# Softmax tails stacked high over low by DMA: two tail passes of 128 rows for three of 104 in a cross-attention and mixture-of-experts kernel

## The chip, the core and the metric

The kernel runs on one core of a Trainium2 chip. Five engines of the core work side by side, each through its own list of instructions, and meet only at semaphores: TensorE (PE) multiplies and transposes, VectorE (DVE) and ScalarE (ACT) read PE's results out of PSUM, GpSimd (POOL) works from SBUF alone, and SyncE (SP) issues the DMA transfers. The metric is the time of one launch on the device in microseconds, the median of three runs.

## What is computed

A layer norm and a cross-attention of 2x1024 rows of width 256 over 154 context rows, with 16 heads of 64, and then a soft mixture of 16 experts with 64 slots each. The part that the change touches is the attention:

```python
q = (x_q @ Wq + bq).reshape(b, sq, H, D_HEAD).transpose(0, 2, 1, 3)
k = (x_k @ Wk + bk).reshape(b, sk, H, D_HEAD).transpose(0, 2, 1, 3)
v = (x_v @ Wv + bv).reshape(b, sk, H, D_HEAD).transpose(0, 2, 1, 3)
s0 = jnp.einsum('bhqd,bhkd->bhqk', q, k) / math.sqrt(D_HEAD)
s0 = jnp.where(mask_mat, NEG, s0)
p = jax.nn.softmax(s0, axis=-1)
s1 = jnp.einsum('bhqk,bhkd->bhqd', p, v)
return s1.transpose(0, 2, 1, 3).reshape(b, sq, D_MID) @ Wo + bo
```

After it the feed-forward part takes a softmax over rows and one over slots of the same logits, runs a gated two-layer network in each expert, and adds the combined result to x.

## The kernel before

**Split operands.** Every matrix is held as two fp32r halves, the rounded value ("high") and what the rounding left ("low"). A product is three passes: high by high, low by high, high by low (`PASSES`, `LEFT_LAST`). For each result in PSUM ACT writes the high half into SBUF, DVE subtracts it from the PSUM value and writes the low half, and that frees the PSUM bank.

**Steps of the attention.** The 2048 rows are 8 groups of 256 rows. The 16 heads are 8 pairs, two pairs make a quad, and a step n is one group with one quad: 8 groups of 4 quads are 32 steps. The events of a step, (name, n, ...), stand in `STEP`, and the queue of PE follows it: S00 to S11 (scores of a pair and a row tile; L1461), Q0, Q1 (queries of the next step; L1439), T0, T1, T2 (transposes of the probabilities of step n-1), PV0, PV1 (probabilities by values of step n-2, one event for each pair), and once in four steps xT and Y0, Y1, the product with Wo (48 matmuls, L1369). R0 and R1 are a reciprocal on DVE and two multiplications on POOL. The tables `LATER_DVE`, `LATER_ACT`, `LATER_POOL` move an event by so many places in that engine's queue; `EARLY` puts single pieces of work ahead of a named event: the projections of keys ("K", pair), of values ("V", batch, half), of the value tails ("VT", half), and the splits of the weights.

**Tails.** A head has 154 keys: 128 and a tail of 26. The main parts of a head's probabilities go through T0 and T1 as 128x128 transposes. The tails of the four heads of a quad go together: `prob_t` holds 4x26 = 104 columns, T2 transposes them (L1479), ACT and DVE write the halves `pT[0]` and `pT[1]` (tile 4), and in each PV event three of the nine matmuls (L1501) multiply `vt`, the value tails of the quad with the other heads' columns at zero, by them: 104 rows each, high by high, low by high, high by low.

**SP's queue.** SP issues its DMAs in one order: first the loads in `LOADS`; then, as they come up, the key blocks of pairs 2 to 7 (L607, two DMAs each, `kbd<-keys`) and, after the last value tail ("VT", 1), eight DMAs that spread the value tails into `vt` (L600, four for each batch); then the second batch's x (L609), the two norm vectors (L610, L611) and, after the last V event, Wo (L614), 1 MB each for x and Wo. Each DMA waits on SP only for what stands ahead of it. The first PV event waits for the first batch's four `vt` transfers (L1492). After that SP has nothing to do in the attention until the slot embeddings are loaded half way through (L617).

## Time and profile before

| | us |
|---|---|
| three runs, median (lowest to highest) | 544.42 (544.23 to 544.68) |
| profiled execution, time / span from first to last instruction | 544.24 / 542.5 |
| PE, PE weight load, DVE, ACT, POOL busy | 530.0, 499.8, 434.1, 402.2, 303.3 |
| load and projections, up to the first Y | 0 to 66 |
| steady attention | 66 to 262 |
| end of the attention, second norm | 262 to 296 |
| logits, slots, experts, combine | 296 to 542.5 |

The time of a launch is the span and 1.7 us around it. A busy share counts an engine as at work from the start of an instruction to its modelled end; what the order of the work costs is read from the chain of waits, which goes back from the last instruction to what released it, and from the rows on what PE waited for.

### The profile page before, as it was taken

To read this page: it belongs to the slowest core of one execution; us is meant where nothing else is said; L and a number is where in the kernel's file an instruction comes from. 1 tells how busy PE (TensorE), PEld (TensorE's weight loads), DVE (VectorE), ACT (ScalarE), POOL (GpSimd) and SP (SyncE) were. 2 spreads that over 40 slices of the span, in tenths; PEclk is the share of its full clock that TensorE was granted. 3 is DMA by queue.
4 is the path that set the end of the run, shared out by engine and by line. 5 is a ranking of instruction groups with operands and counts; after the bars stand their busy time and mean duration, and the time that the engine had idled before them with its cause. 6 is when DMAs were issued, how large, how long until landed. Compare 5 with 4: busy or idle time off the path is not lost.

```text
span 542.5 us, 11967 instructions
## 1 busy us (share of the span) xinstructions
PE 530.0 (98%) x3896; PEld 499.8 (92%) x3896; DVE 434.1 (80%) x1305; ACT 402.2 (74%) x1098; POOL 303.3 (56%) x327
## 2 busy tenths in 40 slices
PE   6999999999999999999998999999999999999997
PEld 4889999999999999999997888999978888899997
DVE  6777878787897979899677998798699888865453
ACT  5879969596896959779564555788979889766562
POOL 6674654544545455454365768787467999910000
DMA  8635000000030000000001333150288888525551
GB/s 257 181 86 179 3 1 2 2 2 1 3 98 2 2 2 1 2 0 4 0 1 80 155 156 156 78 201 1 79 264 283 270 306 288 182 79 170 181 167 67
DMA packets 34901, 54.11 MB, mean 100 GB/s; under 512 B 3997, under 2 KB 21497, under 8 KB 34713
## 3 DMA queue, kind: packets, MB, share of 16 engines
q1 hardware_dynamic: 34841, 53.36, 29.7%
q8 instruction: 32, 0.52, 0.4%
q14 instruction: 28, 0.23, 0.1%
HBM read 40.54 MB, written 10.49 MB: 94 GB/s over the span
## 4 chain that ended last, share of the span: by engine, by line
PE 90%; ACT 4%; DMA 2%; POOL 1%; DVE 1%; issue 1%; SPq 0%; ACTq 0%; DVEq 0%
PE ps L1461 9%; PE ps L1585 9%; PE ps L1357 9%; PE ps L1369 8%; PE ps L1610 8%; PE ps L1499 8%; PE ps L1439 7%; PE ps L1552 7%; PE ps L1476 5%; PE ps L1632 4%; PE ps L1501 4%; PE ps L1644 3%; DMA wvo_raw<-in_L_xattn_Wo_dram 2%; ACT expo L885 1%; PE ps L1615 1%; PE ps L1622 1%
## 5 line engine op out<-in xcount | busy, mean ns | idle before, releaser
L885 ACT ACTIVATE expo<-expo,nmin 128x154 f32<-128x154 f32 x256 | 106.2, 423 | 5.3 <-DVE nmin L1135 4.8
L1135 DVE CUSTOM_DVE_ANT_0 expo<-ps,maskb 128x154 f32<-128x154 f32 x256 | 69.1, 312 | 11.9 <-PE ps L1461 11.9
L723 POOL TENSOR_TENSOR prob_t<-expo,prec 128x104 f32<-128x104 f32 x64 | 23.1, 360 | 89.3 <-DVE prec L1146 89.1
L726 POOL TENSOR_TENSOR prob<-expo,prec 128x512 f32<-128x512 f32 x64 | 66.8, 1043 | 0.0
L1461 PE MATMUL ps<-kbd,qT_high 128*128 128x308 f32 x256 | 61.1, 323 | 0.0
L1155 DVE TENSOR_TENSOR pT_low<-ps,pT_high 128x512 fp32r<-128x512 f32 (+1 forms) x96 | 57.2, 596 | 4.1 <-ACT pT_high L899 3.9
L788 POOL TENSOR_TENSOR w_gu_low<-w_raw,w_gu_high 128x1024 fp32r<-128x1024 f32 x17 | 50.3, 2966 | 16.2 <-ACT w_gu_high L835 16.1
L899 ACT CAST pT_high<-ps 128x512 fp32r<-128x512 f32 (+1 forms) x96 | 49.1, 513 | 10.8 <-PE ps L1476 8.1
L803 ACT ACTIVATE oT_high<-ps,bqv_c 128x256 fp32r<-128x256 f32 x64 | 29.8, 466 | 34.8 <-PE ps L1501 34.7
L885 ACT ACTIVATION_READ_ACCUMULATOR expo<-expo,nmin 128x1 f32 x256 | 50.3, 196 | 0.0
L1461 PEld LDWEIGHTS ps<-kbd,qT_high 128*128 128x128 f32 x256 | 39.8, 190 | 0.2
L1461 PE MATMUL ps<-kbd,qT_low 128*128 128x308 f32 x128 | 39.0, 304 | 0.0
L1476 PE MATMUL ps<-ident,prob 128*128 128x128 f32 x256 | 38.5, 273 | 0.1
L1369 PE MATMUL ps<-wvo_high,oT_high 128*128 128x256 f32 x128 | 37.0, 289 | 0.0
L1501 PE MATMUL ps<-pT_high,vt 104*128 104x256 f32 x128 | 36.3, 284 | 0.0
L1369 PE MATMUL ps<-wvo_high,oT_low 128*128 128x256 f32 x128 | 36.2, 283 | 0.0
L1369 PE MATMUL ps<-wvo_low,oT_high 128*128 128x256 f32 x128 | 36.0, 281 | 0.0
L1357 PE MATMUL ps<-eo_high,comb 128*128 128x256 f32 x256 | 34.6, 287 | 0.4 <-issue 0.4
L1032 DVE SCALAR_TENSOR_TENSOR oT_low<-ps,bqv_c,oT_high 128x256 fp32r<-128x256 f32 x64 | 30.3, 474 | 5.3 <-ACT oT_high L803 4.5
L922 ACT COPY lsb<-ps 128x512 f32<-128x512 f32 x32 | 17.2, 589 | 22.3 <-PE ps L1552 22.3
L1006 ACT CAST comb<-ps 128x512 fp32r<-128x512 f32 x32 | 17.2, 590 | 21.3 <-PE ps L1644 21.3
L1032 DVE SCALAR_TENSOR_TENSOR qT_low<-ps,bqv_c,qT_high 128x256 fp32r<-128x256 f32 x64 | 29.9, 468 | 3.7 <-ACT qT_high L803 3.6
(241 smaller groups left out, 1762.7 us busy)
## 6 DMA issues: line engine op xcount, KB each, us to landing
logits_dram<-lsb SPq DMA_DIRECT2D x16, 512.0 KB, 2.6
w_raw<-in_L_ffn_Wg_dram SPq DMA_DIRECT2D x16, 512.0 KB, 4.0
w_raw<-in_L_ffn_Wu_dram SPq DMA_DIRECT2D x16, 512.0 KB, 4.5
w_raw<-in_L_ffn_Wd_dram SPq DMA_DIRECT2D x16, 512.0 KB, 4.5
lraw<-logits_dram SPq DMA_DIRECT2D x13, 512.0 KB, 3.8
out_dram<-gate SPq DMA_DIRECT2D x16, 128.0 KB, 2.2
kbd<-keys SPq DMA_DIRECT2D x12, 154.0 KB, 2.8
wvo_raw<-in_L_xattn_Wv_dram SPq DMA_DIRECT2D x2, 512.0 KB, 7.0
```

The costliest lines, as they stand in the source:

```text
L726: pool.tensor_tensor(prob[:, n % 2, :, heads, :], expo[:, n % 2, pp, :, :, 0:P], prec[:, n % 2, pp].unsqueeze(3).to_broadcast([P, 2, 2, P] ...
L788: pool.tensor_tensor(low, w_raw[:, i % RAW].rearrange("p (k n) -> p k n", k=KD if w == 0 else FT), high, ALU.subtract).then_inc(low_made(e ...
L885: ins = act.activation(row, row, ACT.Exp, scale=-1.0, bias=nmin[:, n % 2, pp, j, h:h + 1], accum_out=psums[:, n % 2, pp, j, h:h + 1])
L899: act.copy(pT[0][0:rows, n % 2, 2 * t:2 * t + tiles], ps[0:rows, NS + k % NT, 0:tiles * 2 * P].rearrange("p (t n) -> p t n", t=tiles))\
L1032: dve.scalar_tensor_tensor(out=dst, in0=src, scalar=bias, in1=high, op0=ALU.add, op1=ALU.subtract)\
L1135: ins = dve.tensor_tensor_reduce(out=expo[:, n % 2, pp, j, h, :], in0=ps[:, s % NS, h * SK:(h + 1) * SK], in1=maskb[:, (2 * (n // QUADS) + ...
L1155: dve.tensor_tensor(pT[1][0:rows, n % 2, 2 * t:2 * t + tiles], ps[0:rows, NS + k % NT, 0:tiles * 2 * P].rearrange("p (t n) -> p t n", t=ti ...
L1357: ins = pe.matmul(dst[:, 0:D], combT[s][:, i % 2, t], eo[m][:, i // TB, t], start=(first and r == 0 and t == parts[0]), stop=(last and r = ...
L1369: ins = pe.matmul(dst, oT[s][:, p, j * P:(j + 1) * P], wo[m][:, p], start=(first and p == 0 and r == 0), stop=(last and p == PAIRS - 1 and ...
L1461: ins = pe.matmul(dst, qT[s][:, n % 2, pp, j * P:(j + 1) * P], kbd[:, b, m, p, :], start=(r == 0), stop=(r == 2))
L1476: ins = pe.transpose(ps[:, NS + k % NT, (2 * h + j) * P:(2 * h + j + 1) * P], prob[:, n % 2, j, 2 * t + h, 0:P], ident[:])
L1501: ins = pe.matmul(dst[:, 0:2 * P], vt[:, b, s, q, pp * P:(pp + 1) * P], pT[m][0:T4, n % 2, 4], start=False, stop=(r == 2))
```

## The change

Six things change together.

1. The four tails of a quad are kept by pairs: `prob_t` has for each pair 52 columns and 12 of zero, 64 in all, and T2 transposes 128 columns. ACT and DVE write the halves into `tT[0]` and `tT[1]` (one buffer each, not two).
2. SP issues four DMAs a step, `place_tails`: for each pair the 64 rows of the high half and the 64 rows of the low half go into one tile `tS` of 128 rows, one over the other. ACT waits with T2 of step n for the DMAs of step n-1.
3. The value tails `vt` stand per pair, twice over (rows 0 to 63 and 64 to 127), so that one matmul of 128 rows with the high values takes both halves of the probabilities, and a second one with the low values. The three tail matmuls of a PV event are two, at its end, behind a wait for the DMAs (`d_tt`).
4. The DMAs that fill `vt` remain eight, with twice the rows of 256 bytes in each.
5. `STEP`, `PROLOGUE`, `LOADS`, `EARLY` and the three `LATER` tables of the attention have new entries; x, Wk and the mask are loaded ahead of Wq. The product Ya of the last group waits for other PV events.
6. Small moves in the feed-forward part: the first expert's matmuls stand ahead of the last slot transpose (`SLOTS_TAIL`), some biases and exponentials move by some places, and the low half of one more down weight goes from POOL to DVE (`DOWN_DVE`).

```diff
-STEP = "R1 S00 S01 PV0 T0 LN R0 PV1 Q0 XN S10 Q1 T2 S11 T1 xT0 Y0 xT1 Y1"
+STEP = "R1 S00 S01 Q0 PV0 T2 S10 R0 LN Q1 T0 S11 xT0 xT1 PV1 XN T1 Y0 Y1"
 LATER_ACT = {
-    "S": 3.5, "Q": 0.5, "seT": -1, "T": 0.5, "PV0": -1, "S10": 4.5, "S01": 4.5, "T1": -0.5, "Y0": -3,
+    "seT": 0, ("split", WQ, 1): -4.5, ("split", WO, 1): 0.5, ("zeros", 0): -5, ("LN", 0): 0.5,
...
-SLOTS_TAIL = [
-    ("W", 1, 0), ("sT", 15), ("GU", 0), ("W", 1, 1),
-]
+SLOTS_TAIL = [('W', 1, 0), ('GU', 0), ('sT', 15), ('W', 1, 1)]
...
-DOWN_DVE = (3, 6, 9, 12)
+DOWN_DVE = (3, 6, 9, 12, 14)
...
+        def place_values():
+
+            wait_used(sp, LAST_VT)
+            sp.wait_ge(vt_zeros, 3)
+            for b in range(B):
+                for a in range(2):
+                    for twice in range(2):
+                        at = twice * DH + a * TAIL
+                        sp.dma_start(vt[at:at + TAIL, b, :, :, a * DH:(a + 1) * DH]
...
+        def place_tails(ev):
+
+            for half, done in ((0, t_high), (1, t_free)):
+                sp.wait_ge(done, t_no[ev] + 1)
+                for pp in range(2):
+                    to = pp ^ half
+                    sp.dma_start(tS[to * DH:(to + 1) * DH, ev[1] % 2, pp].bitcast(F32), tT[half][pp * DH:(pp + 1) * DH].bitcast(F32))\
+                        .then_inc(d_tt, 16)
+
+        moves = [ev for ev in before_ffn if ev in placed_no or ev == LAST_VT or ev[0] == "T" and ev[2] == 2]
+        first_moves = max(moves.index(ev) for ev in moves if ev[0] != "T") + 1
+        se_at = moves.index(("T", GROUPS // B * QUADS - 2, 2)) + 1
+        for at, ev in enumerate(moves):
             if ev == LAST_VT:
+                place_values()
+            elif ev[0] == "K":
+                place_keys(ev)
             else:
+                place_tails(ev)
+            if at + 1 == first_moves:
+                sp.dma_start(x1[:, TB:TILES], x_t[:, 1]).then_inc(d_x_second, 16)
+                sp.dma_start(gain[:], norm_g.unsqueeze(0).to_broadcast([P, D])).then_inc(d_gain, 16)
+                sp.dma_start(shift[:], norm_b.unsqueeze(0).to_broadcast([P, D])).then_inc(d_gain, 16)
+
+                wait_done(sp, LAST_V)
+                sp.dma_start(wo[2], Wo.rearrange("(k p) n -> p k n", p=P)).then_inc(d_w[WO][0], 16)
...
+                if t == 2 and n:
+
+                    act.wait_ge(d_tt, 64 * n)
...
-                both = max(t_no["T", n, pp], t_no["T", n, 2]) + 1
-                pe.wait_ge(t_high, both)
+                k = t_no["T", n, pp] + 1
+                pe.wait_ge(t_high, k)
...
-                    ins = pe.matmul(dst[:, 0:2 * P], vt[:, b, s, q, pp * P:(pp + 1) * P], pT[m][0:T4, n % 2, 4],
-                                    start=False, stop=(r == 2))
+                pe.wait_ge(d_tt, 64 * (n + 1))
+                for s in range(2):
+                    ins = pe.matmul(dst[:, 0:2 * P], vt[:, b, s, p, :], tS[:, n % 2, pp], start=False, stop=(s == 1))
                 ins.then_inc(acc_full, 1)
```

The new order shows at two places. The first is PE's queue at the first PV event, (PV, 0, 0), with the semaphores that each row waits for (`t_high` and `t_free`: the halves of the probabilities; `d_tails0`: the four `vt` transfers of the first batch). Before:

```order
L1499 MATMUL ps<-pT_high,vm_high 128x256 [waits vm_zeros,d_tails0,acc_free,t_high]
L1499 MATMUL ps<-pT_high,vm_high 128x256
L1501 MATMUL ps<-pT_high,vt 128x256
L1499 MATMUL ps<-pT_high,vm_low 128x256 x2
L1501 MATMUL ps<-pT_high,vt 128x256
L1499 MATMUL ps<-pT_low,vm_high 128x256 [waits t_free]
L1499 MATMUL ps<-pT_low,vm_high 128x256
L1501 MATMUL ps<-pT_low,vt 128x256
```

And in the changed kernel, up to the transposes of the next step's tails:

```order
L1559 MATMUL ps<-pT_high,vm_high 128x256 [waits vm_zeros,d_tails0,acc_free,t_high]
L1559 MATMUL ps<-pT_high,vm_high 128x256
L1559 MATMUL ps<-pT_high,vm_low 128x256 x2
L1559 MATMUL ps<-pT_low,vm_high 128x256 [waits t_free]
L1559 MATMUL ps<-pT_low,vm_high 128x256
L1563 MATMUL ps<-tS,vt 128x256 [waits d_tt]
L1563 MATMUL ps<-tS,vt 128x256
L1539 MATMUL ps<-ident,prob_t 128x128 [waits tail_ready,t_free]
```

Nine matmuls are eight; the tail matmuls moved behind the six others and behind a wait for DMAs, and T2 of the next step follows them at once instead of six events later.

The second place is SP's queue from the key blocks on. Before:

```order
L607 DMA kbd<-keys 64x4x154 x12
L600 DMA vt<-tails 26x8x64 x8
L609 DMA x<-in_x_dram 128x2048
L610 DMA gain<-in_L_ffn_norm_g_dram 128x256
L611 DMA shift<-in_L_ffn_norm_b_dram 128x256
L614 DMA wvo_raw<-in_L_xattn_Wo_dram 128x8x256
L617 DMA se<-in_L_ffn_slot_embeds_dram 128x8x256
```

And in the changed kernel:

```order
L640 DMA kbd<-keys 64x4x154 x10
L649 DMA tS<-tT_high 64x256 x2
L649 DMA tS<-tT_low 64x256 x2
L640 DMA kbd<-keys 64x4x154 x2
L630 DMA vt<-tails 26x16x64 x8
L663 DMA x<-in_x_dram 128x2048
L664 DMA gain<-in_L_ffn_norm_g_dram 128x256
L665 DMA shift<-in_L_ffn_norm_b_dram 128x256
L668 DMA wvo_raw<-in_L_xattn_Wo_dram 128x8x256
L649 DMA tS<-tT_high 64x256 x2
L649 DMA tS<-tT_low 64x256 x2
```

The tails of step 0 moved in ahead of the last key block and of the `vt` transfers; the tails of step 1 and of every later step stand behind x, the norm vectors and Wo.

## Rows read from the trace of the kernel before

**Rows 1.** The page: busy us (share of the span) xinstructions; chain, share of the span.

```profile
PE 530.0 (98%) x3896; PEld 499.8 (92%) x3896; DVE 434.1 (80%) x1305; ACT 402.2 (74%) x1098; POOL 303.3 (56%) x327
PE 90%; ACT 4%; DMA 2%; POOL 1%; DVE 1%; issue 1%; SPq 0%; ACTq 0%; DVEq 0%
```

**Rows 2.** Busy us by stretch: PE, PEld, DVE, ACT, POOL; PEclk, DMA share, GB/s.

```profile
42.00:44.00 2.00, 2.00 (x19) 2.00 (x18) 1.27 (x6) 2.00 (x11) 0.97 (x1) 1.00 0.77 279
110.43:116.80 6.37, 6.37 (x54) 6.37 (x54) 5.64 (x26) 6.17 (x25) 2.19 (x4) 1.00 0.00 0
...
66.00:262.00 196.00, 195.92 (x1608) 195.70 (x1607) 166.39 (x728) 153.65 (x574) 94.79 (x159) 1.00 0.03 8
```

**Rows 3.** Chain in order of time, one steady step: start us, us, what.

```profile
110.43 0.84 PE ps L1461 x6
...
111.50 0.12 PE ps L1501
...
112.34 0.44 PE ps L1476 x4
...
113.86 0.71 PE ps L1439 x6
114.58 0.43 PE ps L1461 x3
...
115.72 0.22 PE ps L1479 x2
...
116.80 0.86 PE ps L1461 x6
```

**Rows 4.** Order of time on PE: the last VT, and the first PV event.

```profile
31.21 0.68 PE L1417 MATMUL ps<-wvo_low,cT_tails_high 128*52 128x512 f32 x2
31.72 0.45 PE L1461 MATMUL ps<-kbd,qT_high 128*128 128x308 f32 x2
39.24 0.48 PE L1499 MATMUL ps<-pT_high,vm_high 128*128 128x256 f32 x2
```

**Rows 5.** Order of time on SP: start us, us in which so many DMAs were issued.

```profile
33.38 7.16 SPq L600 DMA_DIRECT2D vt<-tails  x8
40.58 0.53 SPq L609 DMA_DIRECT2D x<-in_x_dram  x1
42.10 0.67 SPq L614 DMA_DIRECT2D wvo_raw<-in_L_xattn_Wo_dram  x1
```

**Rows 6.** Order of time on ACT: T2's high half in a steady step.

```profile
116.21 0.39 ACT L899 CAST pT_high<-ps 104x256 fp32r<-104x256 f32 x1
```

**Rows 7.** Issue time of one DMA on SP: ns min/median/max; then landing of L607.

```profile
L607 SPq DMA_DIRECT2D kbd<-keys x12: 590/610/1367, 17.9 to 31.0; - x12
DMA to landing us min/median/max: 2.6/2.8/3.3
L600 SPq DMA_DIRECT2D vt<-tails x8: 832/832/996, 33.4 to 39.7; - x8
```

**Rows 8.** Chain in order of time, loads and first steps: start us, us, what.

```profile
8.50 3.44 PE ps L1400 x12
...
15.65 1.94 PE ps L1400 x12
...
34.42 2.79 PE ps L1417 x12
```

**Rows 9.** DMA issues: KB each, median us from issue to landing.

```profile
x<-in_x_dram SPq DMA_DIRECT2D x1, 1024.0 KB, 5.0
...
wvo_raw<-in_L_xattn_Wo_dram SPq DMA_DIRECT2D x1, 1024.0 KB, 9.5
...
sc_b<-in_L_ffn_scale_dram SPq DMA_DIRECT2D x1, 0.5 KB, 5.1
```

**Rows 10.** What PE waited for from 40 to 62 us: us in total, times, longest.

```profile
PE ps L1499 <- ACT pT_high L899: 1.1, 2, 0.8
```

**Rows 11.** What PE waited for from 255 us: the same columns.

```profile
PE ps L1593 <- DVE slot_f L1267: 0.7, 1, 0.7
```

More of the change, by code:

```diff
@@ L136, in attention_schedule @@
     order = []
+    at = STEP.split().index
+    assert at("R1") < at("R0") and at("S00") < at("S01") and at("S10") < at("S11") and at("PV0") < at("PV1")
+    assert at("Y0") < at("Y1")
     for n in range(steps + 2):
@@ L166, in later, with counted @@
     return [order[i] for i in sorted(range(len(order)), key=lambda i: (at[i], i))]
+def counted(order, *numbers):
+    order = list(order)
+    for no in numbers:
+        at = [i for i, ev in enumerate(order) if ev in no]
+        for i, ev in zip(at, sorted((order[i] for i in at), key=no.get)):
+            order[i] = ev
+    return order
 def in_order(order, *numbers):
@@ L377, in program @@
     loop = ExitStack()
-    pT = halves(loop, "pT", [P, 2, 5, 2 * P])
+    pT = halves(loop, "pT", [P, 2, 4, 2 * P])
+    tT = halves(loop, "tT", [P, 2 * P])
+    tS = sb(loop, "tS", [P, 2, 2, 2 * P], F32R)
     oT = halves(loop, "oT", [P, PAIRS, 2 * P])
@@ L514, in wait_done, with last_xT @@
         eng.wait_ge(acc_full, acc_no[ev] + 1)
+    def last_xT(g):
+        return max((("xT", g, k) for k in range(KD)), key=acc_no.get)
     def low_made(e, w):
@@ new lines, in place_keys @@
+        def place_keys(ev):
+            wait_used(sp, ev)
+            for h in range(2):
+                at = slice(h * DH, (h + 1) * DH)
+                sp.dma_start(kbd[at, :, :, ev[1], h * SK:(h + 1) * SK].rearrange("p b s k -> p (b s) k").bitcast(F32),
+                             keys[at, placed_no[ev] % NK].rearrange("p b s k -> p (b s) k").bitcast(F32)).then_inc(d_keys[ev], 16)
+        def place_tails(ev):
[5 more added lines that the diff above has]
+                        .then_inc(d_tt, 16)
@@ L1153, in step @@
                     keys_over(dve)
-                rows, tiles = (P, 2) if t < 2 else (T4, 1)
-                dve.tensor_tensor(pT[1][0:rows, n % 2, 2 * t:2 * t + tiles],
-                                  ps[0:rows, NS + k % NT, 0:tiles * 2 * P].rearrange("p (t n) -> p t n", t=tiles),
-                                  pT[0][0:rows, n % 2, 2 * t:2 * t + tiles], ALU.subtract).then_inc(t_free, 1)
+                dst, high, tiles = [half[:, n % 2, 2 * t:2 * t + 2] for half in (pT[1], pT[0])] + [2] if t < 2 else \
+                    [tT[1][:].unsqueeze(1), tT[0][:].unsqueeze(1), 1]
+                dve.tensor_tensor(dst, ps[:, NS + k % NT, 0:tiles * 2 * P].rearrange("p (t n) -> p t n", t=tiles),
+                                  high, ALU.subtract).then_inc(t_free, 1)
             elif ev[0] == "PV":
@@ L1496, in step @@
                     if m == 1:
[L1497 removed]
+                        pe.wait_ge(t_free, k)
                     for h in range(2):
```

150 lines of the change are left out of this document (74 added, 76 removed).

## The prediction, made blind

> **What bounds the kernel now.** I read the page's table of busy time first: PE is at work for 530.0 of the 542.5 us of the span, and the chain of waits lies on PE for 90% of it [rows 1]. Then the table by stretch: from 66 to 262 us PE is busy for 195.92 of 196.00 us, at a granted clock of 1.00, and ACT for 153.65 [rows 2]. In the steady attention a matmul taken from PE is therefore time taken from the launch, as long as nothing else is late. Then the chain in order of time over one step: scores begin at 110.43 and the next step's at 116.80, so a step without the product Y takes 6.37 us, and one tail matmul 0.12 [rows 3]. Last the two queues in order of time where the attention begins, since there the change puts new transfers into SP's queue behind old ones [rows 4, 5].
>
> The sum is made against the profiled execution (544.24 us, span 542.5). It lies 0.2 below the median of the runs, 544.42, and the forecast is given as it stands; about 0.2% of the time, 1.1 us, is what a measurement can tell from no change.
>
> **Removed: 64 tail matmuls.** There were 3 in each of 64 PV events, there are 2: 64 x 0.12 = **-7.7 us** [rows 3]. T2 transposes 128 columns where it had 104; it is the same 2 matmuls, so nothing. A step without Y becomes 6.13 us. ACT is busy for 6.17 of a step's 6.37 us [rows 2], records that overlap a little counted once, so it could just become the limit in those steps; over four steps with their Y it has 22% to spare (153.65 of 196.00), so I take the gain whole.
>
> **Added: a chain of DMAs in each step.** After T2 comes ACT's half, DVE's half, four DMAs on SP, and their landing, before the last two matmuls of PV. The nearest DMA from SBUF to SBUF is a key block's: 0.60 us to issue with 4 inner rows (the median shows 0.61), 2.8 to land; a `vt` transfer with 8 takes 0.83 [rows 7]. The line through the two is 0.06 us a row, so one row costs some 0.43 to issue, and a landing is about 2.8 - 0.6 = 2.2 us after the end of the issue. The chain is then 0.4 for ACT's half [rows 6] and as much for DVE's, 4 x 0.43 for the issues, of which the first two lie beside DVE's half, and 2.2: between 3.9 and 4.7, about 4.0 us. By the order the tail matmuls stand 5.7 us of PE's work behind T2, added up from the step's durations [rows 3]: nothing in the steady steps, with 1.7 us in hand.
>
> **Added: a wait at the first two steps.** Count from t0, the end of VT's matmuls, 31.72 in the trace [rows 4]. The work of PE from there to the first PV is scores 0.43, Q 0.72, T 0.44, two V 2.78, scores 0.43, T 0.44, scores 0.86 and Q 0.72 [rows 3, 8], so PV(0, 0) is due at t0 + 6.8; before it came at 39.24, t0 + 7.5 [rows 4]. It waits for four `vt` transfers. Their issue began at 33.38, t0 + 1.7, one every 0.90 us (8 in 7.16) [rows 5]; behind the key block and step 0's tails I put it at t0 + 2.0. Each now has 16 inner rows: if that costs nothing the pitch p stays at 0.90, if issue time goes with the rows it is 1.73, and by the line of above it is 1.30 and a gap of 0.06. I take **1.36**, and 0.90 and 1.73 for the range. The fourth lands at 2.0 + 4p + 2.2, so the first wait is 4p - 2.6: **2.8 us (1.0 to 4.3)**.
>
> SP issues x at t0 + 2.0 + 8p = 12.9 (9.2 to 15.8), then the norm vectors and Wo, and only then the tails of step 1. Before, x was issued at 40.58 and Wo, issued at 42.10, landed 9.5 us later [rows 5, 9], 11.0 after the issue of x. Do small transfers stand behind these? The scale, 0.5 KB behind a load of 1 MB, took 5.1 us, and x by itself 5.0 [rows 9]; so I take it that they do. The four tails are 256 KB, about 1.0 us at 279 GB/s [rows 2], and land 12.0 us after the issue of x: t0 + 24.9 (21.2 to 27.8). PV(1, 0) needs them 7.3 us of PE work behind PV(0, 0): two PVs 1.92 and T2, two scores events, Q, T, x's transpose, T, scores, Q and most of a PV, from the same rows [rows 3], so at t0 + 6.8 + 7.3 and the first wait = 16.9 (15.1 to 18.4). The second wait is **8.0 us (6.1 to 9.4)**, and both are **+10.8 (7.1 to 13.7)**. Nothing else of PE can run meanwhile: its queue is in order. ACT stands at T2(2) behind the same transfers.
>
> **PE's restart.** The first twelve key matmuls, after a start with little work, take 3.44 us, the same twelve at 15.65 take 1.94 [rows 8]. After a standstill of 8 us I add the whole difference, **+1.5 (0 to 1.5)**.
>
> The Trainium skill speaks of this on its page "DMA: Bandwidth & Descriptors", in "Queues, rings and completion order": descriptors are consumed in ring order on each engine, though a later one can finish its write ahead of an earlier one. The scale's 5.1 us agrees with the first half; by the second half the tails could pass Wo, and that is rival A's time.
>
> **Smaller parts.** The waits of 1.1 us for ACT at the first PVs [rows 10] are partly gone with the new order: **-0.6 (-1.1 to 0)**. The prologue loads Wk ahead of x and puts the statistics of the norm ahead of DVE's first halves, but warms PE up later: **+0.3 (-0.7 to +1.5)**, bounded by half of the slow start above on one side and the whole on the other. At the end of the attention, where the last steps have no scores to cover anything, tails(31) have an estimated 4.2 us, added up from the order with the same durations [rows 3], before PV(31) needs them, against a chain of 4.0; and the chain of the last probabilities goes through ACT there, so PE's saving buys less: **+0.5 (-1.7 to +2.0)**, a few matmuls either way. The first expert's matmuls ahead of the last slot transpose fill the 0.7 us for `slot_f` [rows 11]: **-0.7 (-0.7 to 0)**. The rest (the down weight from POOL to DVE, the moved biases and exponentials, the wider zeros of `vt`) I cost at nothing: PE hides it, with 98% of the span [rows 1]; uncovered, a half of one weight would be some 3 us on DVE, and no row puts it there.
>
> **Sum:** -7.7 + 10.8 + 1.5 - 0.6 + 0.3 + 0.5 - 0.7 = +4.1, so 544.2 + 4.1 = **548.3 us**. The bounds added as root of the sum of squares are -4.7 and +3.5: 543.5 to 552.
>
> **Rival A: the small transfers are not held behind the big ones.** Then step 1's tails land as soon as they are issued: x's 12.9, 1.52 to Wo's issue, 0.67 for it [rows 5], 1.7 for four issues, 2.2 to land, t0 + 19.0. The second wait is 2.1 and not 8.0 us, and there is no slow restart: 548.3 - 5.9 - 1.5 = about **541.0**. Against it: the 5.1 us of the scale; for it: that load and the scale are different shapes from the tails.
>
> **Rival B: and the wider `vt` transfers cost no more to issue.** With p at 0.90 the waits are 1.0 and 15.3 - 15.1 = 0.2, the sum -7.0: **537.2**. Here the change does what it removes and little more. For it: twice 26 partitions x 16 rows is still one instruction; against it: issue time differs between 4 and 8 rows [rows 7].
>
> **Rival C, slower for good: the tails are late in every step.** If the four transfers take turns, the chain is 0.8 + 4 x 2.2 = 9.6 us against 5.7, and every one of some 28 steps waits. It decides from 5.7 us on; each 0.1 us past that is 2.8 us in all, so 0.5 us late, 14 us over the main case's sum, gives **562**. Against it: key blocks are issued 0.6 us apart, and each lands in 2.6 to 3.3 [rows 7], so two do overlap.
>
> The Trainium skill has a rule for this, on the same page under "Rules for kernel authors": two transfers to disjoint halves of the partitions run one after the other, and one transfer over 128 partitions is to be preferred. Read strictly it gives rival C's time; the trace's pairs of key blocks speak against so strict a reading.
>
> **How the numbers follow.** Main case 0.64, A 0.17, B 0.10, C 0.05, and 0.04 for what I don't name (ACT becoming the bound at 6.05 to 6.2 us a step, which gives back most of the 7.7, among it). The predicted time is the main case's. The range must hold 8 in 10: the main case with 543.5 to 552 and A with 541 and 3 to either side make 0.81, so **538.0 to 552.0**; B and C are left out. Faster by over 0.2% (under 543.3): B 0.10, A 0.14, the main case's lower edge 0.03, the rest 0.02, **0.29**. Within 0.2%: main 0.08, A 0.03, rest 0.01, **0.12**. Slower: **0.59**.
>
> **What would show it right or wrong.** In the profile of the changed kernel, what PE waited for between 40 and 62 us should name a DMA at the first PV (about 2.8 us) and a DMA of `tS` at PV(1, 0) (about 8); SP's queue should show 1.3 us for a `vt` issue, and the tails of step 1 landing at Wo's time. A landing of 2 to 3 us there is rival A; 0.83 us for a `vt` issue, B. A steady step should take 6.13 us, with no PE wait on `tS`; such waits in each step are C, and a step above 6.2 with ACT full is the bound I put aside. The wait for `slot_f` should be gone. The forecast is wrong above all if SP reaches x earlier than t0 + 9 or if the tails overtake Wo.

## The result, and the profile after

The changed kernel takes 563.53 us, median of 4 runs (561.15 to 564.75), against 544.55 us (544.23 to 545.21): a ratio of 1.0343, 95% interval 1.0323 to 1.0363. It is slower by 19 us; 548.3 was forecast, with 552.0 as the upper end. The profiled execution took 564.75 us with a span of 563.0, so the two profiles differ by 20.5 us. One execution of the last experiment below, all_mended, took 737.76 us at a granted clock of 0.66 from end to end; it is the one that was profiled there, and neither its time nor its rows are used.

The page of the changed kernel (busy us, share of the span, instructions; then the chain's shares), against [rows 1]: PE is at work for as long as before, though it has 64 matmuls fewer, and the chain has left it for a third of the span.

```profile
PE 529.9 (94%) x3832; PEld 496.7 (88%) x3832; DVE 445.8 (79%) x1307; ACT 403.7 (72%) x1098; POOL 300.1 (53%) x326
PE 65%; DVE 14%; ACT 5%; issue 5%; DMA 4%; SPq 4%; POOL 2%; ACTq 0%; DVEq 0%; POOLq 0%
```

Where the 20.5 us lie is told by a few marks in PE's queue. The stretches are: up to the first scores; from there to the first Y; four groups of four steps; the two groups in which DVE also norms the slot embeddings; the end of the attention with the second norm and the logits; slots and experts; the combine. All numbers are us, from PE's rows in order of time.

| stretch | before | after | difference | forecast |
|---|---|---|---|---|
| to the first scores | 17.4 | 21.9 | +4.5 | +0.3 |
| to the first Y | 48.5 | 56.8 | +8.3 | +10.7, with the first steps' matmuls |
| Y of group 0 to Y of group 4 | 126.9 | 123.7 | -3.2 | -3.8 |
| to Y of group 6 | 63.7 | 65.7 | +2.0 | -1.9 |
| to the first slot matmul | 83.9 | 88.0 | +4.0 | -0.5 |
| to the first combine matmul | 139.4 | 144.2 | +4.8 | -0.7 |
| to the end | 62.8 | 62.7 | 0 | 0 |

The first two rows come to +12.8 for a forecast of +11.0, by other terms; the third is 0.6 us short of its saving, and the three behind it got longer where they should have got shorter. What PE waited for in the changed kernel up to 70 us (us in total, times, longest); in the kernel before no wait there is longer than 1.9, and [rows 10] is all of it from 40 to 62 us:

```profile
PE ps L1563 <- DMA tS<-tT_low: 5.6, 1, 5.6
PE ps L1442 <- DMA ctx_tail<-in_ctx_dram: 4.2, 1, 4.2
PE ps L1497 <- DVE xT_low L1087: 2.5, 2, 1.4
PE ps L1559 <- DVE qT_low L1089: 2.0, 1, 2.0
```

The second and the third are the prologue's. The last names the wrong instruction. The `qT_low` that it is put down to ends at 44.64, just before the first PV begins at 44.83, but the count of freed banks that this event waits for was full at 43.12: without the transfers PE would have stood for 0.3 us, from 42.8 on. What ended the wait is the landing of the fourth `vt` transfer. SP's queue in order of time (start, us for so many) shows eight issues in 7.14 us, the fourth done at 42.8; its last packet ends at 44.21, 0.63 us ahead of the PV. In the nine kernels below that have the changed STEP and a profile to be read, this packet ends between 42.1 and 46.8 us, and the PV begins 0.62 to 0.65 us behind it in each.

```profile
39.18 7.14 SPq L630 DMA_DIRECT2D vt<-tails  x8
46.37 1.86 SPq L663 DMA_DIRECT2D x<-in_x_dram  x1
48.27 0.42 SPq L664 DMA_DIRECT2D gain<-in_L_ffn_norm_g_dram  x1
48.74 0.43 SPq L665 DMA_DIRECT2D shift<-in_L_ffn_norm_b_dram  x1
49.21 0.64 SPq L668 DMA_DIRECT2D wvo_raw<-in_L_xattn_Wo_dram  x1
49.90 1.35 SPq L649 DMA_DIRECT2D tS<-tT_high  x2
51.30 1.33 SPq L649 DMA_DIRECT2D tS<-tT_low  x2
```

One `vt` transfer still takes 0.89 us with twice the rows [rows 5]. The tails of step 1 follow Wo, as foreseen. Wo was issued at 49.21 and landed at 58.50, the four tails between 58.34 and 59.37, and the chain (start, us, what) goes through the last of them: 64 KB that took 7.35 us to land.

```profile
52.02 7.35 DMA tS<-tT_low
59.37 0.04 issue
59.41 0.80 PE ps L1563 x2
```

Behind each of the two waits PE works slowly, and a third time behind a wait of 3.0 us at the end of the attention (below). By stretch (us; PE, PEld, DVE, ACT, POOL busy; granted clock, DMA share, GB/s), against a granted clock of 1.00 in all of the kernel before:

```profile
44.83:48.69 3.86, 3.86 (x20) 3.86 (x20) 0.57 (x5) 1.56 (x6) 0.00 (x0) 0.58 0.38 92
...
59.00:66.00 7.00, 6.58 (x33) 6.59 (x34) 3.03 (x13) 3.63 (x13) 1.36 (x2) 0.56 0.16 37
...
290.19:293.93 3.74, 3.74 (x19) 3.74 (x20) 0.94 (x3) 0.94 (x3) 3.47 (x5) 0.54 0.00 0
```

From 59 to 66 us PE does 33 matmuls, near the lower of its two levels (1.2 of 2.4 GHz), after a standstill of 5.6 us. From 59.41 to 65.54 it needs 6.1 us for work of 3.4; behind the first wait, 44.83 to 48.69, 3.9 for work of 2.3; behind the third 3.7 for work of 2.2.

The slow work behind the first wait cost the launch nothing, since PE came so much later to tails that were not there yet. In ffn_tables_as_before and slot_norm_in_y below, which have the same queue on SP, the clock does not fall behind the first wait; there the second is 6.9 and 6.7 us and not 5.6, and the first Y comes after the same 56.8 and 56.7 us.

### The profile page after: what moved, and what is told of

It reads as the page before. It is cut to its first block, busy times and chain, and to the rows that moved or that the text cites. A ratio compares the mean times of both kernels' runs of the same rounds, so it can differ in the third digit from the quotient of the medians.

```text
span 563.0 us, 11973 instructions
## 1 busy us (share of the span) xinstructions
PE 529.9 (94%) x3832; PEld 496.7 (88%) x3832; DVE 445.8 (79%) x1307; ACT 403.7 (72%) x1098; POOL 300.1 (53%) x326
## 4 chain that ended last, share of the span: by engine, by line
PE 65%; DVE 14%; ACT 5%; issue 5%; DMA 4%; SPq 4%; POOL 2%; ACTq 0%; DVEq 0%; POOLq 0%
PE ps L1415 8%; PE ps L1427 8%; PE ps L1612 7%; PE ps L1645 7%; PE ps L1519 5%; PE ps L1497 5%; PE ps L1670 5%; PE ps L1559 4%; DMA tS<-tT_low 3%; PE ps L1536 3%; PE ps L1692 3%; PE ps L1704 2%; PE ps L1563 2%; DVE expo L1193 2%; SPq L649 1%
## 5 line engine op out<-in xcount | busy, mean ns | idle before, releaser
L940 ACT ACTIVATE expo<-expo,nmin 128x154 f32<-128x154 f32 x256 | 106.1, 420 | 42.8 <-DVE nmin L1193 42.7
L1193 DVE CUSTOM_DVE_ANT_0 expo<-ps,maskb 128x154 f32<-128x154 f32 x256 | 70.3, 312 | 22.7 <-PE ps L1519 21.1
L1519 PE MATMUL ps<-kbd,qT_high 128*128 128x308 f32 x256 | 64.4, 336 | 0.0
L843 POOL TENSOR_TENSOR w_gu_low<-w_raw,w_gu_high 128x1024 fp32r<-128x1024 f32 x17 | 48.4, 2847 | 20.4 <-ACT w_gu_high L890 20.3
L1214 DVE TENSOR_TENSOR pT_low<-ps,pT_high 128x512 fp32r<-128x512 f32 x64 | 43.2, 675 | 5.0 <-ACT pT_high L957 4.9
L957 ACT CAST pT_high<-ps 128x512 fp32r<-128x512 f32 x64 | 36.7, 573 | 0.0
L1100 DVE TENSOR_TENSOR w_gu_low<-w_raw,w_gu_high 128x1024 fp32r<-128x1024 f32 x14 | 29.1, 2078 | 6.6 <-ACT w_gu_high L890 6.6
L858 ACT ACTIVATE qT_high<-ps,bqv_c 128x256 fp32r<-128x256 f32 x64 | 29.7, 464 | 5.3 <-PE ps L1497 4.8
L890 ACT CAST w_gu_high<-w_raw 128x1024 fp32r<-128x1024 f32 x31 | 31.3, 1057 | 2.2 <-DMA w_raw<-in_L_ffn_Wu_dram 2.2
```

Source lines behind the costliest of these rows:

```text
L843: pool.tensor_tensor(low, w_raw[:, i % RAW].rearrange("p (k n) -> p k n", k=KD if w == 0 else FT), high, ALU.subtract).then_inc(low_made(e ...
L858: act.activation(dst, src, ACT.Identity, bias=bias).then_inc(acc_high, 1)
L940: ins = act.activation(row, row, ACT.Exp, scale=-1.0, bias=nmin[:, n % 2, pp, j, h:h + 1], accum_out=psums[:, n % 2, pp, j, h:h + 1])
L1193: ins = dve.tensor_tensor_reduce(out=expo[:, n % 2, pp, j, h, :], in0=ps[:, s % NS, h * SK:(h + 1) * SK], in1=maskb[:, (2 * (n // QUADS) + ...
L1214: dve.tensor_tensor(dst, ps[:, NS + k % NT, 0:tiles * 2 * P].rearrange("p (t n) -> p t n", t=tiles), high, ALU.subtract).then_inc(t_free, 1)
L1519: ins = pe.matmul(dst, qT[s][:, n % 2, pp, j * P:(j + 1) * P], kbd[:, b, m, p, :], start=(r == 0), stop=(r == 2))
```

## Experiments

Most changes were made to a kernel that mends one thing in the changed one, so that effects don't hide each other. Each is read by its stretches first, since two things differ from one execution to the next: how late loads come to the experts (below), and whether the clock falls behind a wait of PE. What a fall costs can be read from wo_norm_later and wo_after_tails, which are the same program up to the end of the attention: from the first scores to the first Y they take 47.0 us, without one, and 48.4, with one. Medians and ratios with their intervals are given for all.

**SP's queue: wo_after_tails.**

```diff
             if at + 1 == first_moves:
+                pass
+            if ev == ("T", 1, 2):
+                wait_done(sp, LAST_V)
+                sp.dma_start(wo[2], Wo.rearrange("(k p) n -> p k n", p=P)).then_inc(d_w[WO][0], 16)
+            if ev == ("T", 5, 2):
                 sp.dma_start(x1[:, TB:TILES], x_t[:, 1]).then_inc(d_x_second, 16)
...
-                wait_done(sp, LAST_V)
-                sp.dma_start(wo[2], Wo.rearrange("(k p) n -> p k n", p=P)).then_inc(d_w[WO][0], 16)
```

> The changed kernel with only SP's queue altered: Wo is issued behind the tails of step 1, and the second batch's x and the norm vectors behind those of step 5. Theory 1 (the tails of step 1 landed at 59.4 us because SP's queue had put them behind 2 MB of x and Wo): the wait of 5.6 us at the second tail pass goes, and with it the slow matmuls behind it (6.1 us for work of 3.4), so 8 us less, about 555 us; the wait of 2.0 us at the first PV event stays, since it is for the value tails. Rival (it is the traffic, not the place in the queue): the tails of steps 2 to 7 then land late beside Wo and x, PE waits there, and the time stays within 2 us of 563.

553.64 us, ratio 1.0183 (1.0155 to 1.0211). From the first scores to the first Y it takes 48.4 us, 8.4 less; the kernel before 48.5. Theory 1 was right, and the wait at the first PV stays, 2.1 us. The tails of step 1 are issued 2.4 us earlier than in the changed kernel and land before PE needs them. What PE waits for tails over the whole launch is this, 0.7 of it at 255 us:

```profile
47.51 1.18 SPq L649 DMA_DIRECT2D tS<-tT_high  x2
48.79 1.18 SPq L649 DMA_DIRECT2D tS<-tT_low  x2
50.01 0.59 SPq L666 DMA_DIRECT2D wvo_raw<-in_L_xattn_Wo_dram  x1
```

```profile
PE ps L1565 <- DMA tS<-tT_low: 0.9, 2, 0.7
```

And the granted clock from 59 to 66 us is back (same columns as above):

```profile
59.00:66.00 7.00, 7.00 (x58) 6.81 (x57) 5.50 (x25) 6.93 (x24) 5.10 (x5) 1.00 0.19 42
```

So it was the place in the queue. The same megabyte of Wo right behind the tails of step 1 holds nothing up.

**The prologue: prologue_and_wo and wo_loads_prologue.** The first takes PROLOGUE, LOADS, EARLY and the prologue's single entries of the LATER tables from the kernel before, the second PROLOGUE and LOADS alone.

```diff
-    ("split", WK, 0), ("x",), ("bias",), ("split", WK, 2), ("split", WK, 1), ("mask",), ("split", WQ, 0),
-    ("split", WQ, 1), ("split", WQ, 2), ("split", WV, 0), ("split", WV, 1),
+    ("x",), ("split", WK, 0), ("split", WQ, 0), ("bias",), ("split", WK, 1), ("split", WV, 1),
+    ("split", WK, 2), ("split", WV, 0), ("mask",), ("split", WQ, 1), ("split", WQ, 2),
```

> The kernel wo_after_tails and in it also the order of the prologue as before: PROLOGUE, LOADS and EARLY of before, and before's places for single prologue pieces in the three LATER tables. Theory 1 (of the 12.8 us by which the changed kernel is late at its first Y, 4.5 are the prologue's, since the scores begin at 21.9 and not at 17.4, and the rest SP's queue, which wo_after_tails has mended): scores at 17.4, the first Y at 66, 549.5 us. Rival (with scores earlier, PE waits longer for the value tails and the first steps' tails, whose place on SP is bound to other things): the first Y moves by less than 2 us, 552 us or more.

> The kernel wo_after_tails with PROLOGUE and LOADS of before, and all else (EARLY with the value tails' place, the LATER tables) of the changed kernel. prologue_and_wo, with EARLY of before as well, had its scores 4 us earlier but its vt transfers 2.6 us later, at 41.8 us, and its first Y 4.3 us later. Theory 1 (the prologue's 4.5 us lie in the loads' order and PE's, and are there to be had if the value tails keep their place): scores at 17.5 to 18.5, vt issued from 36, first Y at 66 to 67, 550 us. Rival (the LATER tables bind ACT and DVE so that the scores stay behind Wq's halves): scores at 20 or later, 552 us or more.

559.85 us (1.0278, 1.0231 to 1.0325) and 556.97 us (1.0239, 1.0173 to 1.0305). In the first, scores begin at 17.6 us, so the 4.5 us are the prologue's, but not all of them its order's: in the profiles with the changed kernel's prologue the scores begin at 19.8 to 20.9 us where the clock does not fall ahead of them (five), and at 21.7 to 21.9 where it does (three, the changed kernel among them). The order is worth 2.2 to 3.3 us. But with EARLY of before the value tails come later in the new STEP, SP issues `vt` at 41.80 and not at 38.94, and PE stands at the first PV for 5.04 us, and works slowly after it: from the first scores to the first Y 56.7 us, and the first Y is later by 4.3, not earlier. The wait's name here is only "issue"; the end is again the fourth landing.

```profile
41.80 7.15 SPq L611 DMA_DIRECT2D vt<-tails  x8
```

```profile
47.46 0.77 PE L1542 MATMUL ps<-pT_high,vm_high 128*128 128x256 f32 x2 [5.04 <-issue]
```

In the second, scores begin at 21.4: PROLOGUE and LOADS alone bring nothing. PE waits 3.6 us for DVE's `wk_low` there; that the LATER tables, left as changed, hold DVE to the new order is the likely reason, but EARLY was left too, and neither was tried alone. Both rivals were right, the first by more than it said. Prologue, value tails and tables of delays are one schedule, and swapping these parts of it brought nothing.

**DVE in the two groups with the slot norm: slot_norm_in_y, wo_and_slot_norm, wo_no_slot_norm.** The 13 pieces (SA, SB) stand one in a step. The first puts them beside the Ys of groups 3 to 6 (with 0 for SA and SB in `LATER_DVE`):

```diff
-    for k, ev in enumerate(norms):
-        head.insert(head.index(("Q", GROUPS // B * QUADS + 2 + k + (k >= ST // 2), 1)), ev)
+    at_y = {3: norms[0:5], 4: norms[5:8], 5: norms[8:11], 6: norms[11:13]}
+    for g, evs in at_y.items():
+        for ev in evs:
+            head.insert(head.index(("Y", g, 1)), ev)
```

The second puts them where they were, with the places of SA and SB in the LATER tables of before:

```diff
-        head.insert(head.index(("Q", GROUPS // B * QUADS + 2 + k + (k >= ST // 2), 1)), ev)
+        head.insert(head.index(("S", GROUPS // B * QUADS + 1 + k + (k >= ST // 2), 0, 0)), ev)
```

The third leaves the eight SB pieces' arithmetic out, so that it computes something else behind the attention:

```diff
-                link(dve.scalar_tensor_tensor(out=se[:, t], in0=se[:, t], scalar=smv[:, t, 0:1], in1=sg_b[:],
...
+                dve.engine_nop().then_inc(se_ready, 1)
```

> The changed kernel with only the slot embeddings' norm moved: its 13 pieces on DVE stand beside the products Y of groups 3 to 6 and not one in each of 13 steps. Theory 1 (from 205 to 265 us DVE is the bound: steps with a piece take 6.6 us, with DVE at work for 6.5 of them, others 6.1): the eight or so long steps take 6.1 to 6.3, about 4 us less, 559 to 560 us. Rival (the steps are long for PE's own order there, the waits for DVE's halves being only where it shows): no change, 563 us, and steps of 6.6 without such a piece.

> The kernel wo_after_tails with the 13 pieces of the slot embeddings' norm where they stood before on DVE and POOL (ahead of a step's first scores). Theory 1 (from 205 to 265 us DVE is the bound whatever the order: 5.5 us of a step and 1.0 for a piece, and more where POOL works beside it): steps with a piece take 6.4 us and not 6.6, 1 to 2 us less, 552 us. Rival (the piece's place is all there is to it): the steps fall to 6.1 and the time by 4 us, 549.6. slot_norm_in_y has shown that beside Y the pieces cost as much.

> The kernel wo_after_tails with the 16 instructions left out on DVE that scale and shift the slot embeddings (8 pieces, 1.40 us each there, 0.97 in the kernel before); what it computes in the feed-forward part is so another thing, of the same size. Theory 1 (DVE is the bound in the eight steps that hold a piece): these steps fall from 6.6 to 6.1 us, and 3 to 4 us are saved between 205 and 265 us. Rival (the steps are long because of the order of the transposes on PE, and DVE's pieces fill idle time): less than 1 us.

567.15 us (1.0433, 1.0407 to 1.0460), 556.09 us (1.0225, 1.0208 to 1.0242) and 553.07 us (1.0176, 1.0134 to 1.0217). The two groups take 65.7 us in slot_norm_in_y as in the changed kernel (the steps fall from 6.6 to 6.1, but the two steps that hold a Y's pieces grow from 6.6 to 8.8; the Y that holds all five SA pieces, in the stretch before, costs 4.9 us, and with it the median goes up), 67.4 in wo_and_slot_norm, where neither expectation came, and 62.7 without the pieces, against 66.2 in wo_after_tails, where they stand as in the changed kernel. So the pieces cost 3.5 us of this stretch where the change has them. The medians, 553.07 and 553.64, can't show it: the executions of the two kernels lie 6.0 and 3.3 us apart. What PE waits for from 202 to 268 us in the changed kernel is DVE, where the kernel before has no wait at all in these groups:

```profile
PE ps L1539 <- DVE pT_low L1214: 2.3, 6, 0.5
```

DVE's busy time from Y of group 4 to that of group 6 is the third number after the length.

Without the pieces (wo_no_slot_norm), then with them (wo_after_tails):

```profile
193.00:255.00 62.00, 61.10 (x501) 60.45 (x500) 53.25 (x234) 49.79 (x188) 31.96 (x53) 1.00 0.15 36
```

```profile
193.00:259.00 66.00, 62.79 (x504) 60.92 (x503) 60.13 (x248) 50.40 (x188) 32.57 (x55) 1.00 0.14 33
```

What the pieces cost hangs on what POOL does beside them. The group in the kernel before and in the changed one (mean ns of one, 8 each):

```profile
L1196 DVE SCALAR_TENSOR_TENSOR se<-se,smv,sg_b 128x256 f32<-128x256 f32 x8 | 3.9, 482 | 0.0
```

```profile
L1254 DVE SCALAR_TENSOR_TENSOR se<-se,smv,sg_b 128x256 f32<-128x256 f32 x8 | 6.0, 752 | 0.0
```

In the changed kernel's rows in order of time one of them, on DVE, begins while POOL multiplies probabilities, and takes twice as long; in the kernel before it falls into POOL's pause.

```profile
228.28 0.96 DVE L1254 SCALAR_TENSOR_TENSOR se<-se,smv,sg_b 128x256 f32<-128x256 f32 x1
```

```profile
227.91 1.05 POOL L781 TENSOR_TENSOR prob<-expo,prec 128x512 f32<-128x512 f32 x1
```

```profile
220.41 0.48 DVE L1196 SCALAR_TENSOR_TENSOR se<-se,smv,sg_b 128x256 f32<-128x256 f32 x1
```

POOL is through at 228.96, and the DVE instruction ends 0.28 us later. The Trainium skill, page "SBUF — State Buffer", section "SBUF: two separate sides", says that DVE and GpSimd share one port pair, which is an exclusive lock between a DVE instruction with two inputs in SBUF and a GpSimd instruction that reads SBUF: the one that starts second is blocked for the other's whole instruction. The trace agrees for POOL's wide instructions: of the sixteen such DVE instructions of the changed kernel eight begin beside a multiplication of probabilities, 0.03 to 0.36 us after it, and each of the eight ends 0.28 us behind POOL's; one that begins beside a narrow one of POOL, on `rstd`, takes 0.48 us as it does alone. The mean sum of a pair of instructions is 0.97 us in the kernel before, 1.40 in the changed one and 1.53 in wo_and_slot_norm, in the order of the lengths of the stretch, 63.7, 65.7 and 67.4. Eight pairs at 0.43 us more are 3.5 us; before_less_a_tail_pass, with the pairs at 0.97 and as many matmuls in PE's steps as the changed kernel, takes 62.5 us for the stretch, 3.2 less.

**What the removed matmuls are worth: before_less_a_tail_pass.**

```diff
-                    ins = pe.matmul(dst[:, 0:2 * P], vt[:, b, s, q, pp * P:(pp + 1) * P], pT[m][0:T4, n % 2, 4],
...
+                    if r != 1:
+                        ins = pe.matmul(dst[:, 0:2 * P], vt[:, b, s, q, pp * P:(pp + 1) * P], pT[m][0:T4, n % 2, 4],
```

> The kernel before with one of the three tail passes left out (high probabilities by low values), so its result is a little less exact; all else as it was. Theory 1 (PE bounds the steady steps alone, as the prediction took it): 64 matmuls of 0.12 us less, 7 to 7.7 us, 537 us. Rival (DVE or ACT is next to PE in part of the steps): the eight steps with a slot-norm piece, where DVE is at work for 6.36 of 6.40 us, keep their length, and ACT, at work for 6.05 to 6.17, holds others: 3 to 5 us less, 540 us.

541.16 us, ratio 0.9934 (0.9903 to 0.9966): 3 us (1.8 to 5.3), not 7.7. By stretches: 123.2 for the four groups (-3.7, the whole of 32 x 0.12), 62.5 for the two with the slot norm (-1.2, of 1.9), -0.6 at the end of the attention: 5.7 us up to the slots. The rival's time was right, and of its two reasons DVE; ACT held nothing back. Then 143.6 for slots and experts, 4.2 more than before, with the same program. There PE waits 3.0 us for `hid` and works at a granted clock of 0.57 for the 4 us behind it. The chain leads from `hid` over DVE's and ACT's halves back to one weight load that SP took 1.00 us to issue, and not 0.4, and that landed after 6.27, where the kernel before has 4.5 at the same place:

```profile
428.13 1.00 SPq L645 DMA_DIRECT2D w_raw<-in_L_ffn_Wu_dram  x1
```

```profile
428.13 6.27 DMA w_raw<-in_L_ffn_Wu_dram
```

So even with nothing added, the change's saving on PE reaches the end of the launch by less than half in the median; in the shortest of the five executions, 537.84 us, most of it does.

**The late load: before_shifted, before_shifted_more, less_a_pass_shifted.** These move the moment at which the experts are reached, by idle matmuls in the prologue: 25 for 5 in the first, 80 in the second, 36 in the third.

```diff
-    ("warm", 5), ("mask",), ("warm", 2), ("Q", 0, 0), ("K", 3), ("zeros", 3), ("zeros", 1), ("split", WK, 2),
+    ("warm", 25), ("mask",), ("warm", 2), ("Q", 0, 0), ("K", 3), ("zeros", 3), ("zeros", 1), ("split", WK, 2),
```

> The kernel before with 20 more idle matmuls of 512 columns (0.22 us each) in the prologue, so that everything behind comes some 4 us later and is otherwise the same. Theory 1 (the experts take 85.3 us in the kernel before and 89 to 93 in all others, with the same program in two of them, because a weight load there comes some 2 us late and nothing is in hand; it depends on the moment at which the stage is reached): the experts take 88 to 90 us, with a wait for hid, and the time is 552. Rival (the stage's length has to do with what the attention ahead of it leaves, not with the moment): 85.3 us, and 548.5 in all.

> The kernel before with 75 more idle matmuls in the prologue (0.18 us each by before_shifted), so that the experts begin some 14 us later, at 408 us, where the changed kernel begins them. Theory 1 (a weight load comes late by the moment at which the stage is reached): the experts take 88 to 90 us with a wait for hid, 561 us or more. Rival (it is not the moment): 85.2 us as in before_shifted, 558.

> The kernel before_less_a_tail_pass with 31 more idle matmuls in the prologue, so that its experts begin at 394 us as in the kernel before, with 64 matmuls fewer in the attention. Theory 1 (the moment): 85.3 us for the experts, no wait for hid, the time that of the kernel before, 544. Rival (not the moment, but something that the shorter attention leaves or mere chance in each execution): 88 to 90 us in the experts as without the shift, 546 to 548.

548.17 us (1.0077, 1.0050 to 1.0104), 560.40 us (1.0298, 1.0257 to 1.0340) and 545.94 us (1.0023, 1.0003 to 1.0043). From the first matmul of the first expert to the combine their profiles show 85.2, 86.1 and 86.2 us, against 85.3 before and 89.6 without the shift. The moment is not it: reached 4 or 15 us later, the stage is at most 0.8 us longer. The third's time, 545.94, lies 2 us over the 544 expected: in its profile 1.3 of them come of the idle matmuls, which delay the first Y by 6.7 us where the pass saves 5.4 behind it, and 0.9 of the experts. Its runs from 543.89 to 547.92, and those of the kernel before in the same round from 543.37 to 546.19, say that chance has a part in each execution. What makes a load late stays open.

**The feed-forward tables: ffn_tables_as_before.** The changed kernel with SLOTS_TAIL, FIRST_AT, LOGITS_AT and DOWN_DVE as before.

```diff
-SLOTS_TAIL = [('W', 1, 0), ('GU', 0), ('sT', 15), ('W', 1, 1)]
+SLOTS_TAIL = [("W", 1, 0), ("sT", 15), ("GU", 0), ("W", 1, 1)]
...
-DOWN_DVE = (3, 6, 9, 12, 14)
+DOWN_DVE = (3, 6, 9, 12)
```

> The changed kernel with the tables of the feed-forward part as before (the first expert's matmuls behind the last slot transpose, four down weights on DVE, the biases and exponentials where they were). Theory 1 (the two losses behind 400 us, some 2.6 us where the first expert begins and 2.2 us where w_second is waited for, come of these tables): both go, 4.5 us less, 559 us. Rival (they are an echo of the 15 us lost ahead of them, through loads that come at another time): no change, 563 us, with the same waits for hid and w_second_low.

562.14 us (1.0319, 1.0288 to 1.0349): 1.4 less, where 4.5 was expected. What PE waited for from 300 us on in the changed kernel:

```profile
PE ps L1670 <- DVE w_second_low L1100: 2.9, 2, 1.7
PE ps L1682 <- DVE hid L1351: 2.5, 2, 1.3
```

And from 350 to 500 us here:

```profile
PE ps L1678 <- DVE hid L1347: 2.7, 1, 2.7
PE ps L1649 <- DVE slot_f L1321: 0.7, 1, 0.7
```

The wait for `w_second_low` goes; the 0.7 us for `slot_f` of [rows 11] is back; the wait for `hid` stays, here behind a load of 5.9 us at the same place. The nine profiles with the new tables all show 2.9 us for `w_second_low` and none for `slot_f`, so that 2.2 us are the tables'. The waits for `hid` come on top, 1.2 to 3.4 us in the nine, and some 1.0 to 1.6 us of slow work where the clock falls behind them. By this the changed kernel's 144.2 us for slots and experts are 139.4 + 2.2 + 2.5, and the 143.1 here are 139.4 + 2.7 and 1.0 of slow work: a late load took most of what the old tables gave back. Moved ahead of the last slot transpose, the first expert finds the second weight's low half not yet made by DVE, whose two halves take 6.57 us in the chain there:

```profile
411.57 6.57 DVE w_second_low L1100 x2
```

**The end of the attention: wo_and_tail_end, wo_norm_later.** PE waits 3.0 us there for one `oT_low` (its row, then DVE's, in order of time):

```profile
290.19 0.36 PE L1427 MATMUL ps<-wvo_high,oT_high 128*128 128x256 f32 x1 [3.03 <-DVE oT_low L1089]
```

```profile
286.32 1.60 DVE L1271 TENSOR_SCALAR x2f<-x,mv,rstd 128x256 f32<-128x256 f32 x2
...
289.58 0.47 DVE L1089 SCALAR_TENSOR_TENSOR oT_low<-ps,bqv_c,oT_high 128x256 fp32r<-128x256 f32 x1
```

```diff
-N2_AT = 15
-YA_AT = {(0, 0): 27, (1, 0): 22, (0, 1): 32, (1, 1): 33}
+N2_AT = 19
+YA_AT = {(0, 0): 26, (1, 0): 26, (0, 1): 28, (1, 1): 29}
```

wo_norm_later has the first of the two edits alone.

> The kernel wo_after_tails with the places of the second norm and of the partial products Ya in the attention's end as before. Theory 1 (the one wait of 3.0 us for oT_low ahead of a Ya at the end comes of the new places): it goes, 1.5 to 3 us less, 551 to 552 us. Rival (the last steps' chain over ACT, DVE and the tails' DMAs sets the end anyway): the wait moves to another name, time within 1 us of 553.6.

> The kernel wo_after_tails with the first three pieces of the second norm (N2) four places later among the last events, as before, and the partial products Ya left where the change put them. Theory 1 (PE's wait of 3.0 us for oT_low at 287 to 290 us is two of these pieces, 1.6 and 0.4 us, ahead of that half in DVE's queue): the wait falls to about 1 us and 2 us are saved at the end of the attention. Rival (as in wo_and_tail_end, where both were moved, PE then waits elsewhere for as long): the end of the attention keeps its length.

557.05 us (1.0241, 1.0203 to 1.0279) and 556.25 us (1.0210, 1.0149 to 1.0271). From Y of group 6 to the slots they take 92.0 and 88.2 us, wo_after_tails 86.6. In the first a wait of 3.5 us for POOL's `prob_t` takes the place, in the second the wait is 2.1 and 1.3 for `prob_t` come to it. Behind these waits the clock falls in both, in the first for twice as long as in the second, and in wo_after_tails it does not; at the 1.4 us of a fall, and twice that in the first, that leaves about 89 and 87, an estimate: neither edit gained anything, as the rivals said. The two pieces of the norm ahead of that half are part of the wait, but not what sets the end. What does stays open; that the end is longer than before in all ten profiles with the new order, 86.6 to 92.0 us for 83.9, is shown.

**All at once: all_mended.** wo_after_tails with the prologue's order and loads, the feed-forward tables, and the value tails ahead of a key block on SP.

```diff
+        at_vt = moves.index(LAST_VT)
+        moves[at_vt - 1], moves[at_vt] = moves[at_vt], moves[at_vt - 1]
```

> The kernel wo_after_tails with PROLOGUE, LOADS and the feed-forward tables of before, and on SP the value tails ahead of the sixth pair's key blocks. Theory 1 (the losses add): the gains of wo_after_tails (10), of the loads and the prologue (4) and of the tables (1.4 to 2.3), and 1 of the value tails: 547 to 548, so still no faster than the kernel before, since what the removed matmuls bring (3 us, by before_less_a_tail_pass) is less than what the two stretches where DVE is the bound, and the end of the attention, cost. Rival (a further wait takes what is mended): 551 or more.

556.50 us, the median of three (1.0215, 1.0197 to 1.0233). The rival was right. One part of it was to be expected: PROLOGUE and LOADS alone brought nothing in wo_loads_prologue, 556.97 us, either. Where the rest stands is open, for want of a profile. No version of the changed kernel came down to the kernel before.

## Why the prediction was wrong

Its sign and its first mechanism were right, its size was not: +3.9 was forecast, +19 came.

- **The tails behind x and Wo: the mechanism right, the term mis-sized.** The waits were 5.6 us for 8.0 forecast (6.1 was the lower bound) and 2.0 for 2.8, and the second goes when the queue is mended. Rival A, small transfers that pass big ones, is refuted by the 7.35 us and by wo_after_tails: the first of the four landed 0.16 us ahead of Wo, the last 0.87 behind it. Both terms were too large because the pitch of a `vt` transfer stayed at 0.89 us: the line through 4 and 8 rows doesn't hold, and the tails' transfers, with one row, took 0.60 (median) where the line gave 0.43. That the first wait is not the 1.0 us of a pitch of 0.90 has another reason, not in the sum: SP began the `vt` transfers 3.2 us behind t0 and not 2.0. Nearness to 2.8 is in part luck.
- **PE's restart: mis-sized.** 1.5 us was taken as the most. Of the two slow stretches of the start, 1.5 and 2.7 us, only the second reached the launch, but it went on for 6 us where the first twelve key matmuls had stood for 3.4; and a third standstill, at the end of the attention, cost 1.5 more.
- **The prologue: failed step.** +0.3 with an upper bound of +1.5, from the slow first matmuls; it was +4.5, of which 2.2 to 3.3 us are the order's. The new order of loads, pieces and delays was read as a small move because PE's own list differed little; the bound should have come from the chain through the loads, which in the changed kernel runs from Wq's load at 5.2 us over ACT and DVE to 17.8, before PE's first queries are through (start, us, what):

```profile
5.20 5.73 DMA wkq_raw<-in_L_xattn_Wq_dram
...
13.75 1.43 DVE maskb L1130
...
17.39 0.43 DVE xT_low L1087
```

  Which link of this chain brought the loss no run shows.
- **The steady steps: right where PE is alone.** 6.08 us a step for 6.13, and behind the start no wait for `tS` over 0.2 us: so no rival C. ACT is at work for all of it, as the prediction thought possible, and PE as well:

```profile
98.24:104.31 6.07, 6.07 (x53) 6.07 (x52) 5.52 (x26) 6.07 (x25) 2.73 (x4) 1.00 0.19 47
```

- **The gain taken whole: failed step.** The argument was ACT's 22% to spare over four steps, and DVE wasn't asked. In the groups with the slot norm DVE was at work for 6.33 of 6.40 us before, and for 6.55 of 6.60 after (kernel before, then changed):

```profile
217.30:223.70 6.40, 6.40 (x54) 6.40 (x53) 6.33 (x28) 6.07 (x24) 2.73 (x4) 1.00 0.00 1
```

```profile
223.70:230.30 6.60, 6.26 (x52) 6.09 (x51) 6.55 (x29) 6.12 (x24) 2.73 (x4) 1.00 0.18 43
```

  One steady step, at 110 us, stood for all 32; the row that would have told was a hundred us further on.
- **The end of the attention: mis-sized.** With the last steps' matmuls -0.5 was forecast, +2.0 at the most without them; it was +4.0. The sum had no wait there for a half that DVE makes; PE stood 3.0 us for `oT_low`, and the slow work behind it was 1.5.
- **Slots and experts: failed step.** -0.7, "PE hides it", for +4.8. The wait for `slot_f` did go, and a wait of 2.9 us for a weight's low half took its place, +2.2 us by the tables; the waits for `hid` behind late loads are the other 2.5, and cost the kernel with only a pass removed 4.2.

The range missed since all its bounds were drawn around terms that had been named. Of the 20.5 us, 10.8 lie in the last three stretches that differ, to which the sum gave -3.1 in all. That the start came within 2 us of its forecast is luck in part: the waits were 3.2 us shorter, and the prologue and the restart longer.

## What to carry to other kernels

Before a saving on the busiest engine is taken whole, look along the whole launch for the stretches in which a second engine is within a few per cent of it: there the saving ends, and what is added there counts in full. A small transfer that is needed soon goes ahead of the megabytes in its queue, or the megabytes wait: moving two loads was worth 8.4 us of the start here, and some 9 of the launch. A table of delays is one schedule: where a change brings a new one, every stretch has to be priced, and putting one part of the old one back mostly moved the wait here.

## What the runs showed of the hardware

What a wait of PE costs beyond itself differs from one execution to the next. In the changed kernel 2.0 us of wait brought 1.5 of slow work, 5.6 us 2.7 and 3.0 us 1.5. After the 5.6 us 33 matmuls took 6.6 us of a stretch of 7 at a granted clock of 0.56; with the wait gone the same stretch held 58, at 1.00. But of nine profiles with a wait of 2.0 to 2.1 us ahead of the first PV the granted clock falls behind it in five and not in four, and behind the 3.0 us for `oT_low` in six of eight; behind waits of 2.6 to 3.0 us for `hid` it falls in all four, and behind those of 1.1 to 1.7 us in slots and experts in none. With it the times spread: wo_norm_later took from 551.96 us, at a mean granted clock of 0.997, to 559.96, at 0.985.

64 KB from SBUF to SBUF behind 2 MB on the same queue landed after 7.35 us (the last of four; the first after 8.44), ahead of the same 1 MB of Wo after 2.0 to 2.1, which is also the median over the launch. The Trainium skill, page "DMA: Bandwidth & Descriptors", section "Rules for kernel authors", says that two transfers to disjoint halves run one after the other. The trace agrees as far as it can tell: of the four transfers issued from 106.8 us on, the packets of each are under way for 0.3 to 0.5 us, one transfer behind the other. Since SP issues them 0.5 to 1.0 us apart, each lands some 2 us after its own issue, and what the halves cost here is two issues for one.

To issue a transfer from SBUF to SBUF took SP 0.60 us (median) for 64 partitions with 1 row each, 0.61 with 4, and 0.83 for 26 partitions with 8 or 16: in these shapes the number of rows didn't set it.
